# Moving TensorE's small products over both images of a pair, and summing the softmax on VectorE

## The reference

```python
q, vf, vb = (v[:, :, :h], v[:, :, h:2*h], v[:, :, 2*h:])     # v = x @ wqv_w.T + wqv_b
k = x[:, :, None, :] * wk[None, None]
a = -sum_w |q[b,s,h,:] - k[b,t,h,:]| / sqrt(64)              # L1 distance of all token pairs
a = concatenate([a, zeros(b, 1, t, h)], axis=1)              # one more entry, 0
a = softmax(a, axis=1)[:, :t]
o = (einsum('bsdh,bshw->bdhw', a, vf) + einsum('bdsh,bshw->bdhw', a, vb)).sum(axis=2)
y = (o * sigmoid(1.702 * o)) @ fanin_w.T + fanin_b;  return x + y
```

## Time and profile before

| | us |
|---|---|
| median of 3 runs | 2540.39 (2538.69 to 2540.77) |
| the profiled execution | 2541.08, with a span of 2539.3 |
| TensorE products busy | 2232.0 (88%) |
| VectorE busy | 2096.2 (83%) |
| GpSimd busy | 1765.2 (70%) |
| ScalarE busy | 1634.4 (64%) |

### The profile page before, as it was taken

The page is one execution under the profiler, slowest core; times in us unless marked ns, Lnnn a source line. Parts: engine busy times, 40 slices in busy tenths (PEclk is TensorE's granted clock), DMA queues, the critical chain, the costliest instruction groups (busy, mean ns, idle before and its releaser), DMA issues.

```text
span 2539.3 us, 48447 instructions
## 1 busy us (share of the span) xinstructions
PE 2232.0 (88%) x13527; PEld 999.4 (39%) x13527; DVE 2096.2 (83%) x2515; ACT 1634.4 (64%) x4156; POOL 1765.2 (70%) x1033
## 2 busy tenths in 40 slices
PE   5567999999468999999999999999999999999978
PEld 3443333333123344433343344434333444343347
DVE  2887777777878888888888888888888888888874
ACT  0324555555247777777777777777777777777756
POOL 0111333333358998998989989989899899899853
PEclk8788999999779999999999999999999999999989
DMA  4300000000011221122112211221221122112201
GB/s 126 74 1 1 1 0 0 0 0 0 0 45 49 54 53 48 49 52 52 48 49 53 52 47 50 53 50 48 50 53 50 47 52 53 48 48 52 53 18 32
DMA packets 151074, 102.04 MB, mean 40 GB/s; under 512 B 43629, under 2 KB 149038, under 8 KB 150895
## 3 DMA queue, kind: packets, MB, share of 16 engines
q1 hardware_dynamic: 150714, 101.37, 16.0%
q10 hardware_dynamic: 316, 0.12, 0.0%
HBM read 10.64 MB, written 4.19 MB: 6 GB/s over the span
## 4 chain that ended last, share of the span: by engine, by line
PE 52%; DVE 24%; issue 12%; ACT 9%; DMA 1%; DVEq 1%; ACTq 0%; POOL 0%; SPq 0%; POOLq 0%
DVE score L1548 19%; PE pp L850 10%; ACT absd L1133 6%; PE pp L658 5%; PE pp L838 4%; PE pp L789 3%; PE pp L739 3%; PE pp L810 3%; PE pp L679 3%; PE pp L683 2%; PE pp L735 2%; PE pp L684 2%; PE pp L680 2%; PE pp L650 2%; PE pp L784 2%
## 5 line engine op out<-in xcount | busy, mean ns | idle before, releaser
L1548 DVE TENSOR_REDUCE score<-pp 128x16 f32<-128x1024 f32 x1280 | 1498.8, 1217 | 214.2 <-PE pp L850 212.8
L1665 POOL TENSOR_TENSOR absd<-absd 128x2560 f32<-128x2560 f32 x635 | 1442.8, 2272 | 162.1 <-ACT absd L1133 122.1
L1133 ACT ACTIVATE absd<-pp 128x512 f32<-128x512 f32 x1280 | 696.0, 598 | 274.2 <-PE pp L838 274.1
L850 PE MATMUL pp<-blocks,pick 128*128 128x512 f16 x2560 | 750.5, 382 | 100.8 <-DVE score L1548 82.1
L838 PE MATMUL pp<-blocks,pick 128*128 128x512 f16 x1280 | 394.8, 382 | 9.3 <-ACT absd L1133 0.5
L850 PEld LDWEIGHTS pp<-blocks,pick 128*128 128x128 f16 x2560 | 196.7, 98 | 467.3 <-DVE score L1548 312.9
L1632 POOL TENSOR_TENSOR absd<-absd,yw 128x512 f32<-128x512 f32 x112 | 142.4, 1271 | 319.0 <-DVE yw L1470 319.0
L1064 ACT ACTIVATE absd<-pp 128x512 f32<-128x512 f32 x256 | 150.8, 596 | 148.1 <-PE pp L680 145.7
L1486 DVE SCALAR_TENSOR_TENSOR absd<-pp,absd 128x512 f32<-128x512 f32 x256 | 172.4, 687 | 53.3 <-ACT absd L1064 38.4
L838 PEld LDWEIGHTS pp<-blocks,pick 128*128 128x128 f16 x1280 | 114.7, 97 | 207.1 <-ACT absd L1133 59.8
L1163 ACT ACTIVATE expd<-attn 128x65 f32<-128x65 f32 x512 | 162.9, 337 | 0.0
(11 more groups left out here) (234 smaller groups left out, 2721.9 us busy)
## 6 DMA issues: line engine op xcount, KB each, us to landing
blocks<-qk SPq DMA_DIRECT2D x1032, 64.0 KB, 2.0
attn<-score SPq DMA_DIRECT2D x256, 64.0 KB, 2.2
xs<-xn SPq DMA_DIRECT2D x66, 32.0 KB, 1.8
big<-in_wrb_t SPq DMA_DIRECT2D x1, 2064.0 KB
big<-in_x_rows SPq DMA_DIRECT2D x4, 512.0 KB, 6.1
token_rows<-big SPq DMA_DIRECT2D x8, 256.0 KB, 2.0
big<-in_L_ffn_w SPq DMA_DIRECT2D x4, 512.0 KB, 10.2
out<-h SPq DMA_DIRECT2D x16, 128.0 KB, 2.0
```

The source lines that it names most:

```text
L850: mm = pe.matmul(ps[bank + n], pick[:, unit % 8 + n, :], blocks[:, b, unit // 16, unit // 8 % 2, :], start=True, stop=True)
L1133: nc.scalar.activation(absd[odd][:, 16 * u + 8 * n:16 * u + 8 * n + 8, :], ps[4 + n].rearrange("p (h w) -> p h w", w=D), ACT.Abs).then_inc ...
L1548: dve.tensor_reduce(score[:, odd, b, 16 * d:16 * d + 16], pp[:, bank:bank + 2, :].rearrange("p n (h w) -> p (n h) w", w=D), AX.X, ALU.add, ...
L1665: nc.gpsimd.tensor_tensor(x[:, :, 0:w], x[:, :, 0:w], x[:, :, w:2 * w], ALU.add).then_inc(X["tree"], 1)
```

## The change

TensorE: `values_b` and `values_f` move from the first image of the next pair (behind k 0 and k 5) to the end of the second image of their own pair (k 11 and k 14). `sum_e` moves from k 11 to k 5 and `turn_e` from k 13 to k 7 of the first image; `turn` goes from k 8 to 9, `queries` from 10 to 11, `low` from 12 to 13. In the second image `low` goes from k 0 to 1 and `turn_attn` from 5 to 4; `turn_y` moves from k 1 of the next pair to k 15; `fan_in` goes from k 4 to 1. `turn` now waits for `etaken`, and `sum_e` for `sum` in place of `etaken`. ScalarE: its queue follows the new order, and the eight exponentials with accumulators become one activation over 520 elements behind the second image's third A unit. VectorE: `reciprocals` first sums the 8 x 65 exponentials with a reduction and waits for it, and stands behind D1's reduction; `finish` stands behind D2's.

```diff
@@ TensorE
             def turn(p, at):
-                if at >= 3:
-                    pe.wait_ge(X["sum"], p - 3)
-                if at == 2:
-                    pe.wait_ge(X["etaken"], p - 2)
+                if at >= 1:
+                    pe.wait_ge(X["etaken"], p - 1)
...
                 if part == 0:
-                    pe.wait_ge(X["etaken"], p + 2)
                     pe.wait_ge(X["attq"], p + 1)
-                    pe.wait_ge(X["xTq"], 2 * p + 8)
...
-            def sum_e(p, first):
+            def sum_e(p, at):
                 pe.wait_ge(X["abs"], 4 * NA * (p + 1))
-                if not first:
-                    pe.wait_ge(X["etaken"], p)
+                if at >= 3:
+                    pe.wait_ge(X["sum"], p - 1)
...
                     if b == 0:
-                        if k == 0 and at >= 1:
-                            values_b(q - 1, 1 - odd, at)
                         if k == 1 and at >= 3:
-                            turn_y(q - 3)
-                        if k == 4 and at >= 3:
                             fan_in(q - 3)
                         if k == 5 and at >= 1:
-                            values_f(q - 1, 1 - odd)
-                        if k == 8:
+                            sum_e(q - 1, at)
+                        if k == 7 and at >= 1:
+                            turn_e(q - 1)
+                        if k == 9:
                             turn(q + 1, at)
-                        if k == 10:
+                        if k == 11:
                             queries(q + 1, at)
-                        if k == 11 and at >= 1:
-                            sum_e(q - 1, at == 1)
-                        if k == 13 and at >= 1:
-                            turn_e(q - 1)
-                        if k == 12:
+                        if k == 13:
                             low(q + 1, 1 - odd, 0)
                         if k == 14:
                             keys(q + 1, 1 - odd)
                     else:
-                        if k == 0:
+                        if k == 1:
                             low(q + 1, 1 - odd, 1)
                         if at >= 2:
-                            if k == 5:
+                            if k == 4:
                                 turn_attn(q - 2)
                             if 7 <= k < 10:
                                 attend(q - 2, odd, k - 7)
+                        if k == 11:
+                            values_b(q, odd, at)
+                        if k == 14:
+                            values_f(q, odd)
+                        if k == 15 and at >= 2:
+                            turn_y(q - 2)
@@ ScalarE
-                for n in range(2 * part, 2 * part + 2):
-                    op = nc.scalar.activation(expd[:, n, :], attn[:, :, n], ACT.Exp, scale=-(float(D) ** -0.5),
-                                              accum_out=zst[:, 0, n:n + 1])
-                if part == 3:
-                    op.then_inc(X["exp"], 1)
+                nc.scalar.activation(expd[:], attn[:].rearrange("p s n -> p n s"), ACT.Exp,
+                                     scale=-(float(D) ** -0.5)).then_inc(X["exp"], 1)
...
             def pair(q, odd, at):
                 absolute(s, 0, 0, q, first)
-                if at >= 1:
-                    values_b(q - 1, 1 - odd, at < 3)
-                if at >= 3:
-                    turned_y(q - 3)
                 absolute(s, 0, 1, q, first)
                 if at >= 1:
-                    values_f(q - 1, 1 - odd)
+                    copy_e(q - 1)
                 absolute(s, 0, 2, q, first)
+                if at >= 1:
+                    take_e(q - 1, 1 - odd, at - 1)
                 prepare_x(q + 1, 1 - odd)
                 absolute(s, 0, 3, q, first)
                 high_q(q + 1, False)
-                if at >= 1:
-                    copy_e(q - 1)
                 absolute(s, 0, 4, q, first)
                 low(q + 1, 0)
-                if at >= 1:
-                    take_e(q - 1, 1 - odd, at - 1)
                 absolute(s, 0, 5, q, first)
+                high_k(q + 1)
                 s += 1
-                high_k(q + 1)
+                absolute(s, 1, 0, q, first)
                 low(q + 1, 1)
-                absolute(s, 1, 0, q, first)
                 absolute(s, 1, 1, q, first)
                 if at >= 2:
                     turned_attn(q - 2)
                 absolute(s, 1, 2, q, first)
                 if at >= 1:
-                    exponentials(q - 1, 0, at == 1)
+                    exponentials(q - 1, at == 1)
                 absolute(s, 1, 3, q, first)
                 if at >= 2:
                     gate_o(q - 2)
-                if at >= 1:
-                    exponentials(q - 1, 1, at == 1)
+                values_b(q, odd, at < 2)
                 absolute(s, 1, 4, q, first)
-                if at >= 1:
-                    exponentials(q - 1, 2, at == 1)
                 absolute(s, 1, 5, q, first)
-                if at >= 1:
-                    exponentials(q - 1, 3, at == 1)
+                values_f(q, odd)
+                if at >= 2:
+                    turned_y(q - 2)
@@ VectorE
             def reciprocals(p):
                 dve.wait_ge(X["exp"], p + 1)
+                dve.tensor_reduce(zst[:, 0, :], expd[:], AX.X, ALU.add).then_inc(X["zsum"], 1)
+                dve.wait_ge(X["zsum"], p + 1)
                 dve.wait_ge(X["attk"], p)
                 dve.reciprocal(zst[:, 1, :], zst[:, 0, :]).then_inc(X["zr"], 1)
...
-                        if b == 0 and d == 0 and at >= 2:
+                        if b == 0 and d == 1 and at >= 2:
                             reciprocals(q - 2)
-                        if b == 0 and d == 3 and at >= 3:
+                        if b == 0 and d == 2 and at >= 3:
                             finish(q - 3, slot)
```

More of the change, by code:

```diff
@@ L281, in build @@
             "xs", "wk_in", "consts", "xT_ps", "xT_sb", "xTq", "q_ps", "k_ps", "qlo_ps", "klo_ps", "half", "tb0", "tb1",
-            "diffD", "diffA", "red", "abs", "tree", "pooled", "e_ps", "esum", "et_ps", "etaken", "spread0", "spread1", "exp", "zr", "attk", "attq_ps", "attq",
+            "diffD", "diffA", "red", "abs", "tree", "pooled", "e_ps", "esum", "et_ps", "etaken", "spread0", "spread1", "exp", "zsum", "zr", "attk", "attq_ps", "attq",
             "o_ps", "tanh", "y", "yT_ps", "yT", "fan_ps", "hx", "sum", "vb_ps", "vb", "vf_ps", "vf")}
@@ L900, in _ @@
             last = PAIRS - 1
-            values_b(last, 1, 4)
-            turn_y(last - 2)
-            values_f(last, 1)
             fan_in(last - 2)
-            pe.wait_ge(X["sum"], last - 1)
-            sum_e(last, False)
+            sum_e(last, 4)
             turn_e(last)
@@ L1152, in take_e, with exponentials @@
                                ps[7][:, 256:288].rearrange("p (g b h) -> p g b h", g=2, b=2)).then_inc(X["etaken"], 1)
[L1154 to L1161, removed]
-                for n in range(2 * part, 2 * part + 2):
-                    op = nc.scalar.activation(expd[:, n, :], attn[:, :, n], ACT.Exp, scale=-(float(D) ** -0.5),
-                                              accum_out=zst[:, 0, n:n + 1])
-                if part == 3:
-                    op.then_inc(X["exp"], 1)
+            def exponentials(p, first):
+                act.wait_ge(X["spread0"], SPREAD * (p + 1))
+                act.wait_ge(X["spread1"], SPREAD * (p + 1))
+                if not first:
+                    act.wait_ge(X["attk"], p)
+                    act.wait_ge(X["zsum"], p)
+                nc.scalar.activation(expd[:], attn[:].rearrange("p s n -> p n s"), ACT.Exp,
+                                     scale=-(float(D) ** -0.5)).then_inc(X["exp"], 1)
             def turned_attn(p):
@@ L1235, in _ @@
             last = PAIRS - 1
-            values_b(last, 1, False)
-            turned_y(last - 2)
-            values_f(last, 1)
             copy_e(last)
@@ L1264, in _ @@
             turned_y(last - 1)
-            for part in range(4):
-                exponentials(last, part, False)
+            exponentials(last, False)
             root(0)
```

## The result

The changed kernel takes 2703.34 us (2701.89 to 2704.09), against 2540.12 before: 6.4% slower, a ratio of 1.0643 with a 95% interval of 1.0627 to 1.066. The profiled execution has a span of 2700.1 us. The forecast was 2685, in a range of 2615 to 2730.

A forecast was written before the change was run, and what follows sets the result against it. No engine is full, so the order of waits sets the pair: 26.75 to 29.23 us. Over 61 pairs that is plus 151, in total plus 152 on 2541.08: 2692, lowered to 2685 for rounding; range 2615 to 2730.

The forecast's parts named there:

- The working unit: Pacing of reduction units D0 to D9 and ScalarE units A0 to A4, E (prime: second image): 29.23 us a pair.
- Part 1: VectorE's sum of 520 exponentials ahead of the reciprocals: 0.69 us, interpolated, so D2's reduction starts at 1.97 instead of 1.13.
- Part 2: ScalarE's single exponential in place of eight: 0.6 us for 2.5, saving 1.9 a pair on an engine with idle time.
- Part 3: First image: `sum_e` behind D3 waits for VectorE's `finish`, delaying D4 and what follows; with Part 1 it costs 1.03 us.
- Part 4: First image's end: queries behind D7, then ScalarE's in-order copies gate `keys`; D7 to D9 takes 4.7 us against 4.57.
- Part 5: Second image's end: both value products and their copy now stand there; D6' to D9' grows from 4.63, plus 1.42 us.
- The sum: Whole pair: 26.75 to 29.23 us, plus 2.48; 61 pairs give plus 151, the total 2692 us.
- The last step: Whole kernel: pieces rounded up more often than down, some 0.15 us a pair, so 2692 was lowered to 2685.
- A: Rival: TensorE's wait for `finish` is covered by a cheap sum; 0.65 to 1.0 a pair less, 2620 to 2645; chance 0.12.
- B: Rival: only TensorE's issue counts, ScalarE chains shrink, `finish` is in time; 2535, or 2490 with the sum hidden; chance 0.07.
- C: Rival: it cancels at 2540 us if the second image's end keeps 4.6 and `finish` is in time; chance 0.03.
- D: Rival: the clock falls to 0.93 with TensorE less busy, products grow by 1.6 us a pair, 2780; chance 0.05.

## Why the prediction was right, point by point

- **The working unit** held: with the changed order it gave 29.23 a pair, and 29.35 was measured in this pair, 29.40 on average. The steps beside the trace, from D1's reduction at 1036.23: D2's reduction at 1.98 (1.97 forecast), `finish` at 3.10 (3.10), `sum_e` at 3.46 (3.36), D7 at 7.64 (7.52), D9 at 12.35 (12.25), D6' at 20.39 (20.29), D9' at 26.45 (26.34). The whole miss of this pair, 0.1, is one step: TensorE needs 0.15 and not 0.05 from the end of `finish` (1039.54) to the first product of `sum_e` (1039.69). That is 7 us over 61 pairs.
- **Part 1, VectorE's sum**: 0.68, forecast 0.69. The interpolation between 64 and 1024 elements was right. The price of 58 cycles plus one per element in the Trainium skill, "VectorE: DVE Perf Modes", section on the TRN2 errata, gives 0.60, 0.08 too low here. The same section of the Trainium skill says that this row comes out too low for a single operation, where about 150 fixed cycles were measured; an estimate with these is 0.70, and the trace's 0.68 agrees.
- **Part 2, the exponential** was mis-sized: 1.16 for a forecast 0.6. Both lay within the bounds, and nothing hung on it, as the 1.33 of idle time behind it shows. The run with eight exponentials confirms that ScalarE's saving is on no path in the changed kernel.
- **Part 3, the wait for `finish`**: forecast 1.03 with part 1; measured 1.15 (D7 at 7.64 for 6.49 in the earlier trace rows). Putting `finish` first took 55.9 us away, where 49 were expected.
- **Part 4, the first image's end**: D7 to D9 4.71, forecast 4.73. `keys` starts at 1047.62, 3.75 behind D7, and stayed on the chain through ScalarE, 0.06 behind the end of the low half's copy:

```profile
1046.95 0.61 ACT L1102 CAST qk<-pp 128x512 f16<-128x512 f32 x1
```

  The run that moves `keys` away from it, from 2540 to 2474.72, shows that of the places tried this was the costliest of the kernel before. The prediction read it and didn't see that it was the way to a better kernel.
- **Part 5, the second image's end**: 6.06, forecast 6.05; alone 99 us, in the kernel before.
- **The sum**: 151 for 61 pairs, measured 159 (29.40 for 26.79 on average from pair 3 on). The first three pairs cost 4.4 us, forecast 4.5. The end of the kernel was to give 3 to 4 back and gave nothing: from the last D9' reduction to the end it is 108.0, before 107.8. And the stage began 2.5 us earlier than before (717.8 for 720.3); over ten of the profiled kernels, all with the same stages ahead of it, that start lies between 717.7 and 720.3, with the changed kernel's relatives from 717.7 to 719.2, so no run ties it to the change. That the early start and the missing gain at the end nearly cancel is luck. The last step, 7 us off for pieces rounded up, went the wrong way: 2692 was nearer.
- **The rivals**: A (the wait is covered) falls with the 1.57 us, B (D7 to D9 in 3.7) with 4.71, C (D6' to D9' in 4.6) with 6.06, and D with a clock that stayed at 1.00 at 85% busy (24.99 of 29.35) and a wait of 1.57. The Trainium skill, "TensorE: Matmul & The Clock Gate", section on HAM oscillation, has the clock fall after longer gaps than these; the trace agrees as far as it goes, with no fall at waits of up to 1.7 us and no longer ones in this stage.

The end of the kernel gave nothing, in part because of an operation that the prediction didn't look at. In the changed kernel, VectorE and GpSimd have these rows in the tail:

```profile
2602.67 3.10 DVE L343 TENSOR_TENSOR absd<-xn 128x1024 f32<-128x1024 f32 x1
```

```profile
2602.34 2.35 POOL L1675 TENSOR_TENSOR h<-h,bo 128x1024 f32<-128x1024 f32 x1 [5.41 <-DVE xn L340]
```

Before, the same two operations started in the other order and VectorE's took 1.22, GpSimd's 3.39. Whichever came second waited for the first: here 1.9 of what was gained went into VectorE's. The rest of that end was not followed up.

## What to carry to other kernels

Room in a queue is no use elsewhere in it: a product is free where its engine would wait for a partner that has work in store, and costs about its length where it stands in a chain through a second engine's queue that its own next instructions wait for (1.6 a pair for the two value products, 1.0 for `keys`). Before moving a step, write the work between two units against what the partner takes for one, and for each moved wait ask which operation signals it and what stands ahead of that operation in its own queue. A piece of work for an engine that is not full is free or not by its place: the same 0.8 us a pair cost 0, 27 or 52 us here.

## What the runs showed of the hardware

One activation over 520 elements from SBUF takes 0.64 us when both sides are flat, 1.16 when it reads with a stride of 32 bytes (8 rows of 65) and 1.15 when it writes with one of 260 bytes (65 rows of 8). That 8 rows and 65 rows cost the same speaks for the stride and against the number of rows, but no run has many rows without a stride. The Trainium skill, "SBUF — State Buffer", section "Door 1: The DMA port swizzle", has SBUF lines of 16 bytes and a price for each access that goes to a new line; the three durations agree with it, but no run here tries a stride below 16 bytes.

A VectorE operation with two inputs in SBUF and a GpSimd addition exclude each other, 3.10 for 1.22 us on the side that comes second, while VectorE's sum with one input takes 0.68 with GpSimd at work beside it. The Trainium skill says both, in the same page's section "Who interferes with whom"; the trace agrees.
